# Expert units listed in two tables, the first of them begun beside the last tiles' sums

## The reference

```python
def _sage_conv(x, edge_index, W_l, W_r, b):
    agg = segment_sum(x[src], dst) / max(degree, 1)
    return agg @ W_l + x @ W_r + b

def _moe(tokens, router_w, w1, b1, w2, b2):
    probs = softmax(tokens @ router_w.T)
    rw, re = top_k(probs, 2)
    rw = rw / max(rw.sum(-1), 1e-12)
    combine = zeros((N, 8)).at[arange(N)[:, None], re].set(rw)
    out = tokens
    for e in range(8):
        h = gelu(tokens @ w1[e] + b1[e], approximate=False)
        out = out + combine[:, e:e + 1] * (h @ w2[e] + b2[e])
    return out

x = x + sage(relu(sage(layernorm(x))))
x = x + _moe(layernorm(x))
```

## Time and profile before

| | us |
|---|---|
| median of 3 runs | 626.25 (624.56 to 627.48) |
| the profiled execution, its own time | 625.75 |
| its span, first to last instruction | 624.0 |
| outside the span | 1.75 |
| PE busy | 556.2 (89%), 3021 matmuls |
| DVE busy | 350.6 (56%) |
| ACT busy | 223.0 (36%) |
| POOL busy | 182.7 (29%) |

### The profile page before, as it was taken

The page is one execution under the profiler, slowest core; times in us unless marked ns, Lnnn a source line. Parts: engine busy times, 40 slices in busy tenths (PEclk is TensorE's granted clock), DMA queues, the critical chain, the costliest instruction groups (busy, mean ns, idle before and its releaser), DMA issues.

```text
span 624.0 us, 11265 instructions
## 1 busy us (share of the span) xinstructions
PE 556.2 (89%) x3021; PEld 331.0 (53%) x3022; DVE 350.6 (56%) x1199; ACT 223.0 (36%) x422; POOL 182.7 (29%) x179
## 2 busy tenths in 40 slices
PE   5999989999999999999999999999920699999992
PEld 3444545555555555554454554544510588877882
DVE  5987656676667667653447576676683123332330
ACT  5766834444444444441001000000000255545542
POOL 4840000000000000000311533444444076567885
PEclk9999999999999999999999999999965699999997
DMA  8421201111111111114522355633317379798994
GB/s 266 128 73 52 93 9 51 52 44 34 51 51 41 37 51 51 34 44 126 188 77 61 130 162 160 189 101 111 108 63 222 107 162 196 165 199 163 193 182 57
DMA packets 70711, 66.86 MB, mean 107 GB/s; under 512 B 12053, under 2 KB 68740, under 8 KB 70670
## 3 DMA queue, kind: packets, MB, share of 16 engines
q1 hardware_dynamic: 55486, 50.61, 27.6%
q0 software_dynamic: 11584, 14.25, 12.2%
q10 hardware_dynamic: 3600, 1.48, 0.9%
HBM read 38.11 MB, written 29.14 MB: 108 GB/s over the span
## 4 chain that ended last, share of the span: by engine, by line
PE 54%; issue 13%; DMA 12%; DVE 10%; POOL 7%; POOLq 2%; ACT 1%; SPq 1%; DVEq 0%; ACTq 0%
PE bank L1242 21%; PE counts_ps L636 6%; PE bank L1232 6%; PE bank L1157 6%; DMA out<-adj 4%; PE counts_ps L1242 4%; PE counts_ps L1384 4%; POOL xs_dram L573 3%; PE bank L1395 2%; DMA adj<-in_L_ffn_w 2%; POOL stat L566 2%; POOL out L609 2%; DMA xs_dram<-onehots 2%; DMA y<-y_dram 2%; DMA xs_dram<-w,onehots 1%
## 5 line engine op out<-in xcount | busy, mean ns | idle before, releaser
L1242 PE MATMUL bank<-y,adj 128*128 128x512 f16 x625 | 154.7, 379 | 0.4 <-ACT zt L1450 0.4
L1242 PE MATMUL counts_ps<-y,adj 128*128 128x512 f16 x625 | 144.3, 379 | 2.1 <-DMA y<-y_dram 2.1
L609 POOL DMA_INDIRECT out<-adj x56 | 87.0, 1554 | 54.3 <-ACT adj L1580 30.6
L643 ACT ACTIVATE adj<-counts_ps 128x1000 f32 (+1 forms) x80 | 80.2, 1004 | 61.1 <-PE counts_ps L636 61.1
L1242 PEld LDWEIGHTS counts_ps<-y,adj 128*128 128x128 f16 x625 | 60.6, 101 | 64.9 <-DMA y<-y_dram 4.0
L1242 PEld LDWEIGHTS bank<-y,adj 128*128 128x128 f16 x625 | 57.8, 97 | 59.5 <-issue 13.7
L554 POOL IOTA onehots<- 128x8 int32 x1 | 0.1, 143 | 232.0 <-PE counts_ps L636 232.0
L1384 PE MATMUL counts_ps<-adj 128*128 128x256 f32 x240 | 59.8, 393 | 4.3 <-DMA adj<-in_L_ffn_w 3.0
L1544 ACT ACTIVATE rows<-bank 128x256 f32<-128x256 f32 x25 | 9.6, 383 | 128.5 <-PE bank L1316 128.5
L636 PEld LDWEIGHTS counts_ps<-onehots 125*128 125x128 f16 x640 | 41.1, 98 | 27.1 <-ACT adj L643 10.9
L622 DVE TENSOR_TENSOR onehots<-iota,lo_t 125x1024 f16<-125x1024 f16 x80 | 54.5, 682 | 0.2
(11 more groups left out here) (230 smaller groups left out, 618.4 us busy)
## 6 DMA issues: line engine op xcount, KB each, us to landing
adj<-in_L_ffn_w SPq DMA_DIRECT2D x38, 256.0 KB, 3.6
adj<-xs_dram SPq DMA_DIRECT2D x31, 264.0 KB, 3.5
rows<-z_dram SPq DMA_DIRECT2D x49, 128.0 KB
z_dram<-zt SPq DMA_DIRECT2D x36, 128.0 KB, 1.7
rows<-in_x SPq DMA_DIRECT2D x24, 128.0 KB
out<-yo SPq DMA_DIRECT2D x24, 128.0 KB
y_dram<-yo SPq DMA_DIRECT2D x23, 128.0 KB, 1.7
y<-y_dram SPq DMA_DIRECT2D x4, 640.0 KB, 6.6
```

The lines of the kernel that those rows point to most:

```text
L609: g.indirect_dma_start(out, bass.IndirectOffsetOnAxis(ap=ids[u][:, h:h + 1], axis=0), ye[u][:, h, :], None, bounds_check=N - 1, oob_is_err ...
L643: nc.scalar.activation(adj[:, :, bass.ds(at, GW * WD)].rearrange("p b (h d) -> p b h d", d=WD), counts_ps[:, 2 * (group % 2):2 * (group % ...
L1242: last = te.matmul(to, adj[:, b, t * P:(t + 1) * P], y[:, b, :], start=(b == 0), stop=(b == NT - 1))
```

## The change

The units are listed in two tables. A first one, `early_units`, is made by DVE between tiles 21 and 22: it lists the full units (256 rows, no padding) of the pairs of the first 20 tiles, rounded down to a whole number of rounds. With these inputs the first 20 tiles hold 1+3+0+4+1+1+2+4 = 16 full units, so the first four rounds are early ones. A second table, `late_units`, is made after all tiles are placed and lists the rest, 12 units in three rounds; the total stays 28 units.

The first round is written out on every engine, woven with the last tiles' steps (`choose`, `shares`, `place`, the last `x2_norm`, the scatters of tiles 20 to 24). Then a loop runs over the other early rounds but one, and a second loop over the rest after a wait for the second table. On SP the row number is now read after the waits and not before them. The order of sums in `out` is kept by a new rule: each half of a unit has its own semaphore, and three tables instead of one say how many units' first halves and second halves must have landed. POOL waits on eight semaphores before each half.

```diff
+    EARLY = 5
+    EARLY_TILES = 20
+    EARLY_MID = 2
-        ye_out = [sem(f"ye_out{u}") for u in range(UNITS)]
+        ye_out = [[sem(f"ye_out{u}{h}") for h in range(2)] for u in range(UNITS)]
...
+            load_w1(0, 0)
+            load_w1(1, 1)
+            sp.wait_ge(S["tok_free"], KEPT + EARLY_TILES)
+            load_rows(0, 0)
+            load_rows(1, 1)
...
-                    row = row_of(i + 3)
                     sp.wait_ge(S["xe_tr"], n * UNITS + (u + 2))
                     sp.wait_ge(S["meta_in"], n * UNITS + (u + 2))
-                    load_rows(row, 1 - s)
+                    load_rows(i + 3, 1 - s)
...
+            def unit_sums(n, u):
+                i = n * UNITS + u
+                before_halves = [pool.value_load(tab_w[h][0:1, bass.ds(i, 1)], min_val=0, max_val=MAX_PAIRS)
+                                 for h in range(2)]
+                before_it = pool.value_load(tab_fi[0:1, bass.ds(i, 1)], min_val=0, max_val=MAX_PAIRS)
+                for h in range(2):
+                    for half in range(2):
+                        units = before_it if h else before_halves[half]
+                        for q in range(UNITS):
+                            pool.wait_ge(ye_out[q][half], (units + (UNITS - 1 - q)) // UNITS * 16 + 16)
+                            pool.sem_inc(S["pool_held"], 1)
+                    pool.wait_ge(S["ye_in"], n * (2 * UNITS) + (2 * u + h + 5))
+                    pool.sem_inc(S["pool_held"], 1)
+                    g.indirect_dma_start(out, ...).then_inc(ye_out[u][h], 16)
+
+            scatter(EARLY_TILES, EARLY)
+            scatter(EARLY_TILES + 1, EARLY)
             pool.wait_ge(S["table"], 1)
             pool.wait_ge(S["u_out"], 16 * NT)
+            unit_sums(0, 0)
+            scatter(EARLY_TILES + 2, EARLY)
+            unit_sums(0, 1)
+            scatter(EARLY_TILES + 3, EARLY + 1)
+            scatter(EARLY_TILES + 4, EARLY + 1, LAST)
+            unit_sums(0, 2)
+            unit_sums(0, 3)
+            with pool.Fori(1, full) as n:
+                for u in range(UNITS):
+                    unit_sums(n, u)
+            pool.wait_ge(S["table"], 2)
+            with pool.Fori(full, rounds) as n:
+                for u in range(UNITS):
+                    unit_sums(n, u)
```

More of the change, by code:

```diff
@@ L504, in _ @@
                     load_w1(i + 2, s)
[L506 to L508 removed]
+            with sp.Fori(1, full) as n:
+                unit_loads(n)
+            sp.wait_ge(S["table"], 2)
+            rounds = sp.value_load(nround_i[0:1, 0:1], min_val=MIN_ROUNDS, max_val=MAX_ROUNDS)
+            sp.wait_ge(S["padded"], 16 * NE)
+            for u in range(UNITS):
+                for h in range(2):
+                    sp.wait_ge(ye_out[u][h], 16)
+            for q in range(2):
+                sp.wait_ge(scattered[q], 16 * TOPK * len(range(q, NT, 2)))
+            with sp.Fori(full, rounds) as n:
+                unit_loads(n)
+            for u in range(UNITS):
+                for h in range(2):
+                    sp.wait_ge(ye_out[u][h], rounds * 16 + 16)
+                    sp.sem_inc(S["held"], 1)
         @block.gpsimd
@@ L1414, in _ @@
                     turn_rows(1 - s, n * 32 + 16 * ((u + 3) // 2 + 1))
+            pe.wait_ge(S["table"], 1)
+            full = pe.value_load(full_i[0:1, 0:1], min_val=MIN_EARLY - 1, max_val=MAX_EARLY - 1)
+            pe.sem_inc(S["ysum_in"], 2)
+            pe.wait_ge(S["ew_in"], 16 * 2 * NE)
+            pe.wait_ge(S["sums_free"], NT - 1)
+            turn_rows(0, 16)
+            pe.wait_ge(S["sums_free"], NT)
+            turn_rows(1, 16)
+            turn_token(NT - 2)
+            hidden(0, 0, 16)
+            score(NT - 2)
+            prefix(EARLY)
+            turn_rows(0, 32)
+            pe.wait_ge(S["sums_free"], NT + 1)
+            hidden(1, 1, 16)
+            result(0, 0)
+            turn_token(NT - 1)
+            hidden(2, 0, 32)
+            score(NT - 1)
+            turn_rows(1, 32)
+            result(1, 1)
+            hidden(3, 1, 32)
+            prefix(EARLY + 1)
+            turn_rows(0, 48)
+            for i in (2, 3):
+                result(i, i % 2)
+                hidden(i + 2, i % 2, 48)
+                turn_rows(1 - i % 2, 16 * ((i + 3) // 2 + 1))
+            with pe.Fori(1, full) as n:
+                unit(n)
+            pe.wait_ge(S["table"], 2)
+            rounds = pe.value_load(nround_i[0:1, 0:1], min_val=MIN_ROUNDS, max_val=MAX_ROUNDS)
+            with pe.Fori(full, rounds) as n:
+                unit(n)
         @block.scalar
@@ L1588, in _ @@
             gelu(1, 1)
-            with act.Fori(0, rounds) as n:
-                for u in range(UNITS):
-                    i, s = n * UNITS + u, u % 2
-                    weigh(i, n, u)
-                    gelu(i + 2, s)
-                    turn_rows(i + 3, 1 - s)
+            phase3(NT - 1)
+            weigh(0, 0)
+            gelu(2, 0)
+            turn_rows(3, 1)
+            weigh(0, 1)
+            gelu(3, 1)
+            turn_rows(4, 0)
+            powers(EARLY + 1)
+            weigh(0, 2)
+            gelu(4, 0)
+            turn_rows(5, 1)
+            weigh(0, 3)
+            gelu(5, 1)
+            turn_rows(6, 0)
+            with act.Fori(1, full) as n:
+                unit(n)
+            act.wait_ge(S["table"], 2)
+            rounds = act.value_load(nround_i[0:1, 0:1], min_val=MIN_ROUNDS, max_val=MAX_ROUNDS)
+            with act.Fori(full, rounds) as n:
+                unit(n)
 _INS = ["x", "src", "dst", "L0_gnn_W1_l", "L0_gnn_W1_r", "L0_gnn_b1", "L0_gnn_W2_l", "L0_gnn_W2_r", "L0_gnn_b2",
```

417 lines of the change are left out of this document (256 added, 161 removed).

## The result

| | before | after |
|---|---|---|
| median, runs on one chip | 626.05 (4 runs) | **692.4** (4 runs, 691.77 to 692.75) |
| span of the profiled execution | 624.0 | 690.1 |
| PE busy | 556.2 (89%) | 578.4 (84%) |
| POOL busy | 182.7 (29%) | 183.0 (27%) |
| start of the first sum on POOL | 500.39 | 485.81 |

After is slower: the ratio to before is 1.106, with a 95% interval of [1.1042, 1.1079]. The first sum does come 14.6 us sooner. The last comes 66 us later. The prediction was slower too, at 672 us; the measured time is 20 us above it and inside its range.

A forecast was written before the change was run, and what follows sets the result against it. POOL's instruction stream was taken as the loop's bound: 480 (first sum) + 171.7 (27 units) + 1.9 (second half) + 2.6 (branches) + 4.4 + 3 (scatters) = 663.6; with 6.5 behind and 1.75 outside, 672 us; range 625 to 695.

The forecast's parts named there:

- POOL's stream: Unit loop: table reads, waits and issues cost POOL's sequencer 6.36 us a unit, 171.7 us for 27 steps.
- The first table: DVE between tiles 21 and 22: 49 added instructions take 11 us, bounds 8 and 14; PE then waits 9 us.
- The last norm: End of DVE's last tiles' steps, before the first sum: reached at 472 us.
- SP hidden under the stream: SP's row read after its waits adds 0.64 us, 4.7 us a unit, hidden under POOL's 6.36.
- PE busy about 65%: Sign in the changed kernel's profile: PE's busy share in the unit loop.
- rival 3: Unit loop: PE's clock falls to its lower level for good, 8.4 us a unit, end 717 us; chance 0.03.
- The first sum: POOL's start of the unit loop: about 480 us, 20 us sooner than before, bounds 472 and 490.
- rival 2: SP's row read sets the pace if POOL's stream is under 4.7 us a unit: 615 us; chance 0.06.
- The first three steps: First units on POOL: 6.36 us each, plus scatters of tiles 22 to 24, 4.4 us of issue and 3 of waiting.
- Waits for other experts' units: POOL in the loop: 15 us before, now beside the longer stream, costed at nothing, bounds 0 and 10 us.
- A round's turn: Each round's branch on POOL's sequencer: 0.44 us, six times, 2.6 us.
- rival 1: POOL's stream stays hidden and the loop keeps its pace: 603 to 611, say 607 us; chance 0.10.

The follow-up runs named there:

- e14: after, with SP reading a unit's row number ahead of its waits, as before does; 692.7 us, ratio 1.1057.
- e3: before, with only a longer stream on POOL: three table reads and sixteen waits with increments a unit; 691.1 us, ratio 1.1049.
- e6: after, with three counts packed into one table that POOL reads once, no increments, no waits on the unit's own semaphores; 650.3 us, ratio 1.0412.
- e9: e6, with SP reading a unit's row number ahead of its waits; 644.3 us, ratio 1.0284.
- e11: e7, with SP reading a unit's row number ahead of its waits; 618.1 us, ratio 0.9855.
- e8: before, with each half unit's sum in a DRAM buffer of its own and no waits for earlier experts' sums; 621.4 us, ratio 0.9915.
- e7: e6, with each half unit's sum in a DRAM buffer of its own and no waits for earlier experts' sums; 627.95 us, ratio 1.0028.
- e1: after, without the sixteen increments of pool_held between a unit's waits, every wait kept; 665.9 us, ratio 1.0637.
- e2: after, with one more table read on POOL for each unit, its result unused; 704.3 us, ratio 1.1248.

## Why the prediction was right in direction and 20 us short

What held, by the prediction's steps:

- *POOL's stream.* 1.9 us between a unit's sums was 1.93, and 4.4 us to the next unit was 4.30 to 4.46, once 4.67, where no wait was blocked and no round began. The pieces were read from the chain of before. The Trainium skill, Runtime: NRT & Kernel Launch, section on instruction fetch mechanics, gives about 20 cycles as a floor for each instruction; the prediction weighed it and went by the trace. The runs go with the trace: 448 increments less gave 26.5 us, 0.059 us for each in the mean and 0.074 where nothing blocked.
- *The first table*: 11 us predicted, 10.4 measured. *PE's wait for it*: 9, measured 8.14. *The last norm*: 472, measured 473.3.
- *SP hidden under the stream*: e14 moved nothing.
- *PE busy about 65%*: 73% between 530 and 610 us, where its matmuls ran at a lower mean granted clock, 0.87 to 0.91; over the whole loop, 490 to 684 us, 62%. That is a piece of rival 3 without its effect: PE had idle time to take it from.

Two slips of arithmetic in the prediction change little: its own parts give 478.2 for the first sum (472, 2.5 and 3.7) and not 480, and 644 for the lower bound and not 643. By rival 2's sum, a stream between 4.7 and 5.1 us gives 615 to 626 us and not 623 to 629.

What failed. The last sum came at 683.79 where the sum of terms had 663.6, 20.2 us:

- *The first sum*, 480, was 485.8: **5.8 us**. The prediction had 2.5 us for the last row of `out` to land, put the scatters of tiles 20 and 21 beside it, and then had 3.7 us of reading. It left out that POOL waits for tile 20's landing behind these scatters: that ended at 480.18, 6.9 us after the last norm had started. The reading, with the number of rounds, and the issue took 5.6 us from there. The whole lies in the given bounds (472 to 490).
- *The first three steps*: 28.4 us (485.81 to 514.21) for 3 x 6.36 + 4.4 + 3 = 26.5: **1.9 us**.
- *Waits for other experts' units, costed at nothing*: 24 steps took 6.98 us each and not 6.36 + 0.1: **12.4 us**. Of these, 8.9 are waits that stood blocked until a sum had landed. This is the step that failed. The argument was that landings run beside the longer stream. At five of the thirteen changes of expert in these steps they do. At the other eight the wait comes too early in the stream: before 556.27 the sequencer was at the fifth wait 2.9 us after its first read (549.66 to 552.57), and the landing took 4.73. With two tables there are 14 changes of expert and not 7. The bound of 10 us for it held.
- The other 3.5 us of the 12.4 are stream that was priced too short. A round's turn was taken as 0.44 us; in e3, the steps into a new round took 6.8 us where the others took 6.1 to 6.5. Unit 12, ahead of which POOL leaves one loop and reads the number of rounds for the next, took 7.64 us with no wait blocked. In units 13 and 25 the second sum came 2.69 us after the first and not 1.93; why is open.

The second thing that failed is in no term of the sum but in rival 1: a hidden stream was to give 607 us. The runs take the change apart like this:

| from | to | what went | us |
|---|---|---|---|
| 692.4 after | 650.3 e6 | POOL's stream made short | 42 |
| 650.3 e6 | 644.3 e9 | SP's row read ahead of its waits | 6 |
| 644.3 e9 | 618.1 e11 | the order of sums in `out` | 26 |
| 621.4 e8 | 618.1 e11 | what the early start gives with all of that gone | 3 |

These are medians of different chips; by the ratios the four steps are 41, 8, 27 and 4 us.

The early start was valued by its first sum, 20 us sooner. It is worth 3 or 4 us in e11 against e8, nothing in after against e3 (692.4 and 691.1), and in e7 against e8 it costs 6.6. For the units that fill PE's gap wait in their turn for the last tiles' work, and what was one gap of PE is now several. With its stream short and everything else in place (e9, 644.3) the kernel is slower than before still.

## What to carry to other kernels

A control instruction on POOL's sequencer cost between 0.06 and 0.6 us and showed in no engine's busy time; before one is added in a loop, its stream per turn is worth adding up from the chain of waits and setting against the pace of the slowest engine. Such a stream lies beside a landing only as far as it stands ahead of the wait for it: what stands behind a blocked wait was paid after it, 1.66 us in after and 1.22 in e6, so numbers should be read and worked out ahead of the first wait that can block. And here work that was started early in a gap was worth not its own lead, but what is left of the lead once the work that it was put in front of has been done.

## What the runs showed of the hardware

- A stream of waits bound the loop on an engine that was 27% busy: POOL's cores had the same 183 us of work in a program 66 us longer.
- The size of it: 0.21 us from one computed wait with its increment to the next, 0.074 us of run time for an increment in steps in which nothing blocked (e1), 0.50 us for a table read (e2), 0.52 us for the issue of an indirect DMA, 4.73 us (after) and 4.83 us (e6) from the start of an accumulating sum to a landing that was waited for, and 5.05 for a plain scatter.
- The granted clock went back and forth between its two levels: 1.00 between 558 and 562 us, 0.50 between 660 and 670, and 0.83 to 0.91 in the mean of the 40 us windows from 490 to 610 us, in which PE was busy for 63 to 74% of the time; before, at 94% busy, it was 1.00. In the last window, from 650 us on, it was 0.60, with PE busy for 22%.
